# Moving four of the twenty halves that stand beside the scores of a four-stage convolution kernel

## The reference, cut to what matters

```python
x = x + patches_experts(gn(x))    # 25 patches of 10x10 per image, each by one of 8 expert 3x3 convolutions,
                                  # chosen by argmax of the patch means @ Wg, gated by softmax
x = x + mixed_conv(gn(x))         # per image: 4 expert kernels mixed by a sigmoid of pooled @ w_route, then 3x3 convolution
x = x + codebook[argmin_k |v - codebook_k|^2] # for each pixel's 32-vector v of gn(x), 512 codewords
x = x + deformable(gn(x))         # offsets = w_grid @ gn(x) + b; 9 taps per pixel sampled bilinearly, then w_conv
```

## Time and profile before

| | us |
|---|---|
| median of 3 runs | 1838.69 (1831.52 to 1839.75) |
| the profiled execution | 1828.76 |
| its span, first to last instruction | 1827.0 |
| busy: PE, DVE, ACT, POOL | 1572.8, 1527.7, 1105.7, 1203.4 |
| mean granted clock of TensorE | 0.952 of full speed |

### The profile page before, as it was taken

One profiled execution on the slowest core, in us unless ns is written; L12 is line 12 of the kernel. 1 busy time (PEld: TensorE's weight loads), 2 busy tenths in 40 slices (PEclk: granted clock), 3 DMA queues, 4 the chain that ended last, 5 costly groups with the idle time before them and its releaser, 6 DMA issues.

```text
span 1827.0 us, 42287 instructions
## 1 busy us (share of the span) xinstructions
PE 1572.8 (86%) x15584; PEld 1289.7 (71%) x15584; DVE 1527.7 (84%) x3113; ACT 1105.7 (61%) x1547; POOL 1203.4 (66%) x1403
## 2 busy tenths in 40 slices
PE   4686389889898999989898998989899899988998
PEld 3644376689666885678666896668866797668997
DVE  5467389989898888989898898988989788988998
ACT  2011366568554775567665676548755677658985
POOL 2043277786677666786677766776677856778764
PEclk9788699999999999999998999999999999999999
DMA  6536875699657976589656986579765895336552
GB/s 138 130 95 161 185 221 163 169 231 227 189 162 195 237 205 181 172 216 224 191 159 169 246 212 200 155 193 242 210 186 159 218 216 157 85 88 171 160 154 70
DMA packets 284244, 326.12 MB, mean 179 GB/s; under 512 B 209444, under 2 KB 223780, under 8 KB 280192
## 3 DMA queue, kind: packets, MB, share of 16 engines
q1 hardware_dynamic: 240712, 228.88, 47.7%
q0 software_dynamic: 35856, 80.87, 17.8%
q10 hardware_dynamic: 7472, 13.67, 2.4%
HBM read 253.50 MB, written 56.40 MB: 170 GB/s over the span
## 4 chain that ended last, share of the span: by engine, by line
PE 43%; DVE 16%; DMA 9%; DVEq 8%; POOL 8%; issue 7%; SPq 5%; ACT 2%; ACTq 1%; POOLq 0%
PE bank L1362 26%; DMA words<-in_codebook,code 5%; PE bank L1490 4%; DVE code L1229 4%; DVEq L1228 4%; POOL fetched L638 3%; PE bank L1444 3%; POOL words L661 3%; DVEq L1023 3%; PE bank L1473 3%; PE bank L1342 2%; DVE samp L1024 2%; SPq L469 2%; DVE weighted L1014 2%; PE bank L1349 2%
## 5 line engine op out<-in xcount | busy, mean ns | idle before, releaser
L638 POOL DMA_INDIRECT fetched<-row_pairs,corner x768 | 742.3, 967 | 378.8 <-issue 201.8
L1362 PE MATMUL bank<-lent,tent 128*128 128x160 f32 x6144 | 941.4, 308 | 5.3 <-issue 4.4
L1362 PEld LDWEIGHTS bank<-lent,tent 128*128 128x128 f32 x6144 | 871.6, 195 | 98.1 <-issue 60.1
L770 ACT ACTIVATE tent<-lent,row_at_sb 128x768 f32<-128x768 f32 x512 | 448.8, 924 | 50.3 <-PE bank L1362 44.9
L774 ACT ACTIVATE tent<-tent 128x1536 f32<-128x1536 f32 x256 | 380.0, 1484 | 20.6
L1006 DVE TENSOR_TENSOR strip<-bank,near 128x480 f32<-128x480 f32 x512 | 331.0, 648 | 43.6 <-PE bank L1362 39.2
L661 POOL DMA_INDIRECT words<-in_codebook,code x256 | 244.8, 956 | 103.6 <-issue 53.1
L1024 DVE TENSOR_REDUCE samp<-strip 128x96 f32<-128x480 f32 x414 | 270.4, 653 | 37.0 <-issue 1.3
L1490 PE MATMUL bank<-cb,xs 64*128 64x512 f32 x512 | 218.1, 658 | 30.1 <-DVE code L1229 15.8
L851 ACT COPY xs<-xn 32x128 f32<-32x128 f32 x256 | 75.5, 295 | 230.9 <-PE bank L1490 213.0
L759 ACT COPY samp_t<-bank 96x384 f32<-96x384 f32 x256 | 119.8, 468 | 152.6 <-PE bank L1349 65.1
(11 more groups left out here) (152 smaller groups left out, 1356.8 us busy)
## 6 DMA issues: line engine op xcount, KB each, us to landing
lent<-z_rows SPq DMA_DIRECT2D x256, 384.0 KB
picked_weights<-arena SPq DMA_DIRECT2D x14, 1800.0 KB
arena<-picked_weights SPq DMA_DIRECT2D x21, 720.0 KB
arena<-windows SPq DMA_DIRECT2D x276, 50.0 KB, 2.0
arena<-xp SPq DMA_DIRECT2D x96, 136.0 KB
fetched<-row_pairs,corner POOLq DMA_INDIRECT x768
arena<-row_pairs SPq DMA_DIRECT2D x64, 160.0 KB
slice<-picked_weights SPq DMA_DIRECT2D x14, 720.0 KB
```

The source lines that it names most:

```text
L638: pool.indirect_dma_start(fetched[:, N % FETCHES, k].rearrange("p q c -> p (q c)"), None, pairs_dram[b % 2], bass.IndirectOffsetOnAxis(ap= ...
L770: act.activation(w[:, piece], zs[:, N % SPREADS, :], ACT.Abs, bias=row_at[:, piece:piece + 1])
L1362: m = pe.matmul(STRIPS[j % 3][:, XW * C * e:XW * C * (e + 1)], tent[:, N % TENTS, c, DENSE * d + e], picture[:, b % 2, i, c], start=(c == ...
```

## The change

```diff
--- before.py
+++ after.py
@@ -70,7 +70,7 @@
 
 
 GROUP_TILES = 32
-SCORE_HALVES = 20
+SCORE_HALVES = 16
 WHOLE = float(3 << 22)
 FAR = 35.0
 MIDDLE = FAR * (NBLK - 1) / 2 + (H + 1) / 2
@@ -292,7 +292,7 @@
         PLACE = {}
         reached = -SHIFT
         for name, many in (("row0", 5), ("row1", 5), ("row2", 5), ("row3", 5), ("y", 5), ("features", 1), ("pool", 4),
-                           ("mix", 2), ("conv1", 1), ("norm2", 2), ("scores", SCORE_HALVES), ("spell", 1), ("pick", 1),
+                           ("mix", 3), ("conv1", 2), ("norm2", 2), ("scores", SCORE_HALVES), ("spell", 2), ("pick", 2),
                            ("norm3", 2), ("rows", 2), ("near", 3)):
             PLACE[name] = (reached, reached + many)
             reached += many
@@ -1513,8 +1513,8 @@
                             turn_route(k)
                         if i == 1 and t == 1 and k:
                             spread_gates(k)
+                at("spell")
                 turn_words(TILES - 2)
-                at("spell")
                 at("pick")
                 keep_running(6)
                 turn_words(TILES - 1)
```

## The result

| | us |
|---|---|
| the changed kernel, median of 6 runs | 1856.11 (1848.23 to 1863.29) |
| the kernel before beside it, median of 6 runs | 1836.17 (1825.3 to 1843.13) |
| ratio | 1.0119 (95% interval 1.0088 to 1.0149) |
| its profiled execution, and span | 1863.29, 1861.4 |
| mean granted clock (before 0.952) | 0.936 |

It is slower by 1.2%, 16 to 27 us of 1836. The forecast of no change within 0.5% was wrong; 1856 lies in the range.

A forecast was written before the change was run, and what follows sets the result against it. DVE was taken as the bound, with POOL 4 us from it in row 0. Per group -6.1 + 1.3 + 4.9 = +0.1 us, x 7 = +1 on 1838.69, put at 1839; own range 1830 to 1848, 8-in-10 range 1815 to 1859.

The forecast's parts named there:

- The forecast of no change within 0.5%: Whole kernel: less taken from DVE comes back as waits for POOL, +0.1 us per group; chance 0.43.
- The scores: Between first and last search: four halves leave, 6.1 us less per group on DVE, with PE not becoming late.
- Behind the last search: From the last search's end to half 53 in row 0: 4.9 us more per group, through POOL's added sums.
- The place of the wait: Behind the last search: L1528 1.2 us later for tile 20's turn, then DVE standing 3.2 us before half 51.
- a 3 us wait before half 51: Sign in row 0: DVE waits 3 us or more; if missing, the forecast is too slow by up to 22 us.
- Mixing and convolution: Weights to first search: third mixing half free, second convolution half 2.6 us less 1.3 for clock, 1.3 us more.
- the first half of the convolution at 2.8 us in nearly all groups: Sign behind the mixing: filled gap holds PE's clock, with PE idle under 1 us before it.
- The lock between VectorE and GpSimd: DVE's weightings beside POOL's sums: the two lock each other out, up to 6 us more; taken as nothing.
- POOL doesn't catch up in the scores: Slower rival: look-ups end later than 2.5 us behind the last search; 1857, or 1866 with low convolution clock; chance 0.25.
- The forecast's own range: Whole kernel: 1830 to 1848 us, from unknown costs above and half the faster rival's gain below.
- the 6 and the 9 us: Unknown costs above the forecast: 6 us for locks between DVE and POOL, 9 for the clock.
- The faster rival: The scores lose their waits for PE's score matmuls and POOL is less late: 19 us less, 1821; chance 0.32.

The follow-up runs named there:

- c: The changed kernel with the words of tile 6 turned ahead of the halves behind the last search, as before: 1852.30 us, ratio 1.0111.
- e: The changed kernel with nine unused matmuls on PE ahead of its wait for POOL's sum of half 41: 1848.82 us, ratio 1.0086.
- g: The changed kernel with tile 20 turned behind L1528 and not ahead of it: 1853.64 us, ratio 1.0098.
- a: The kernel before with only three halves in mixing, two in the convolution and 18 in the scores, old tail: 1824.84 us, ratio 0.9970.
- f: The kernel before with one more half in mixing and 19 in the scores, nothing else: 1824.30 us, ratio 0.9951.
- h: The kernel before with three mixing, two convolution and 18 score halves, and the sum of half 41 on VectorE: 1828.47 us, ratio 0.9973.
- i: The kernel before with the sums of halves 41 and 42 on VectorE and not POOL: 1828.88 us, ratio 0.9981.
- k: The kernel before with one more half in mixing and 19 in the scores, run a second time in five rounds: 1827.42 us, ratio 0.9964.
- b: The changed kernel's tail alone: 18 halves in the scores, mixing and convolution as before: 1861.50 us, ratio 1.0161.
- d: The changed kernel with the sums of halves 39 and 40 on VectorE and not POOL: 1834.47 us, ratio 1.0009.
- j: The changed kernel with the sums of halves 39 to 42 on VectorE and not POOL: 1834.64 us, ratio 1.0009.

## Why the prediction was wrong where it was

**The scores, the step that failed.** "Two of each go from between the first and the last search", 6.1 us. In DVE's order only three halves went: 18 halves (21 to 38) stood between S and T before, 15 (23 to 37) with the change. The fourth had stood behind T already: before there were four halves there (39 to 42) and not three, as I had it also in the section on the change, now five (38 to 42). Three halves, two of them with the weighting, are 1.77 x 2 + 1.30 = 4.8 us by the prediction's own prices. The rest is a wait that I had excluded ("PE ... does not become late"). The words of tile 4 land late, PE stands before their turn, and the strips behind them are late and slow (a half takes 3.35 us there and not 1.75). In the changed kernel, group 5, PE and then DVE:

```profile
1210.56 0.48 PE L1500 MATMUL bank<-ident_sb,words 128*128 128x128 f32 x1 [5.72 <-DMA words<-in_codebook,code]
1210.82 3.35 PE L1362 MATMUL bank<-lent,tent 128*128 128x160 f32 x12
```

```profile
1214.21 0.66 DVE L1006 TENSOR_TENSOR strip<-bank,near 128x480 f32<-128x480 f32 x1 [3.06 <-PE bank L1362]
```

DVE's waits for strips in the scores went from 0.6 to 2.1 us per group. The wait for words is older than the change: before the turn of tile 4's words PE stood 2.3 us on the mean of groups 1 to 7, with the change 3.3, and 2.9 to 3.3 in all six kernels with 16 halves against 0.9 to 2.3 in those with more. So fewer halves give it less cover. Measured: -4.1 in this profile, and -3.6 as the mean of the six kernels with 16 halves (74.6 to 75.8) against the two with 20 (79.0, 78.7).

**Behind the last search: right in size, and in POOL as the limit of most of it.** Forecast, half 53 at T+48.5 in place of 43.6, +4.9. Measured +5.1; over the kernels with this tail, both sums on POOL and 16 halves in the scores (changed, c, e, g) the mean is 48.9, over those with the old one (before, a, f, h, i, k) 44.0, so +4.9. b has the tail too, but its later look-ups, and is left out. Two sums off POOL give back 3.0 of it (d); the other 2 us stay in j as well, and no run gives them to POOL. The marks, forecast and measured in group 4: last look-up's end T+1.3 and T+1.2; sum 41 at T+14.4 and T+14.6; sum 49 at T+45.4, as forecast, on the mean of the groups (T+45.2 in group 4); L1234 at T+7.8 and T+8.2; 119 sums on POOL, as counted.

**The place of the wait was wrong.** I had PE slip by 1.2 us at L1528 and stand before half 51 in row 0. By my own numbers tile 20 would be turned at T+15.1, 1.8 us (not 1.2) behind the image of before (1009.30, T+13.3), and behind everything else that PE had to do; L1528 did start at T+15.3. But I put no wait and no clock behind that. PE idles 2.7 us, and L1528 then runs at a low clock (0.58 on the mean of that stretch), 1.2 us longer on the mean: L1272 is 3.6 us late, so that row 0 starts with its delay, and POOL has caught up by half 51. That a 3 us wait before half 51 would be missing was my own sign for a forecast too slow by up to 22 us. The sign misled: the wait was missing since it had been paid earlier. e brings it back in all seven groups (2.7 to 6.9 us) by filling the first wait, g in three of them, and group 1 of the changed kernel has it too.

**Mixing and convolution.** Forecast +1.3 between weights and first search. The profile shows +3.6, but this stretch moves by 2 us without any edit (16.1 before and 18.2 in i, whose code is the same there). The eight kernels with mix 3 and conv1 2 have 18.85 on the mean, the three with 2 and 1 17.3: +1.5. The sign that I had set, the first half of the convolution at 2.8 us in nearly all groups, came true in part: in five of the eight, before in three. Group 5 and group 6 of the changed kernel:

```profile
1133.81 2.78 PE L1473 MATMUL bank<-arena,mix 96*32 96x512 f32 x24 [1.09 <-DMA arena<-xp]
```

```profile
1351.12 5.35 PE L1473 MATMUL bank<-arena,mix 96*32 96x512 f32 x24 [3.33 <-DMA arena<-xp]
```

PE no longer waits for the mixed weights there, but for the stacked rows (11.1 us in all, before 7.2), and where they land late the clock is low as before.

**The lock between VectorE and GpSimd.** I left at nothing a term bounded by 6 us. The weightings L1014 went from 142.3 to 147.6 us, 5.3 more, and back to 142.4 in j, where POOL makes 91 sums and not 119. The rule of the Trainium skill ("SBUF — State Buffer", who interferes with whom) that spoke against the change is borne out in sign: 16 of the 17 weightings of over 0.75 us ran while POOL was adding, and the 46 that met a sum took 0.69 us on the mean, the other 210 0.55. Its price is near the upper end. How much of it lies on the path was not tried; what falls into the tail is part of the 4.9.

**The sum with measured terms:** -3.6 + 1.5 + 4.9 = +2.8 us per group, x 7 = 20 us; the medians differ by 20. One term makes the miss, the scores (2.5 x 7 = 17 us). The rival "POOL doesn't catch up in the scores", with 1857, came near the time for another reason: its condition, look-ups that end later than T+2.5, was not met (T+1.2). The low clock in the tail was the part of it that came. The condition was met in b (T+2.8), and there half 53 was 1.7 us later, near the 1.85 that it had named. That 1856 lies within 1815 to 1859, 3 us from its end, is thus luck: the width came from this rival and not from the step that failed. The forecast's own range stopped at 1848, and even with the 6 and the 9 us that it names above 1839 it would have stopped at 1854. The faster rival's waits before searches did shrink (11.2 for 16.6 us), but 5 us in all, and the strips' waits took their place.

## What to carry to other kernels

Moving work from a full engine's busy stage to its quieter one removes nothing: it pays only through waits that end. So count, in the engine's own order, on which side of each mark every moved piece stands before and after; one half counted wrongly was 1.3 us of a sum of which every group multiplies the error by seven.

When a helper engine is just in time, find the last point that needs it and work out its arrival there. A wait that you remove upstream (e, g) only shows up there again; taking work from the helper (d) is what moves the end, until taking more no longer helps (j).

A missing wait is no sign that the time is free: look first whether the same lateness was paid at an earlier place.

## What the runs showed of the hardware

- TensorE behind a wait, the same 16 matmuls L1528: 2.00 us after 1.66 us of idle time (d, group 4), but 2.76 to 3.06 after 1.63 to 1.67 in three other groups of d; 3.54 after 2.17 (j) and after 2.68 (changed kernel), but 1.90 after 2.70 in group 1 of the changed kernel; and 1.90 in every group where matmuls filled the wait (e). In the convolution 3.33 us of waiting were followed by 5.35 (group 6), where rows 5 had 2.78 after 3.35. So the idle time just before does not settle the level by itself.
- Of VectorE's 256 weightings (L1014), nearly all of 0.55 us, 17 took over 0.75 us with the change, and 4 before; of GpSimd's last additions (L686), mostly 0.40, 33 of 119 took about 0.65, before 10 of 98.
- A look-up of words by GpSimd can land so late that PE stands 5.72 us for it. Which transfer holds it up was not tried.
